# First-layer projections ahead of the global token, x loaded in halves, padding on VectorE, and a router product of weights, in a four-part transformer kernel

## The reference

```
x = x + attention0(layernorm(x))   # 16 heads of 64, windows of 128, plus one "global" part
x = x + memory(layernorm(x))       # router: top 8 of 512 stored values, scaled by a gate
x = x + attention1(layernorm(x))   # 16 heads of 8, all 2048 keys, rotary
x = x + experts(layernorm(x))      # main network and 2 of 8 experts per 128 tokens
```

## Time and profile before

| | us |
|---|---|
| median of 3 runs (1297.92, 1299.36, 1327.26) | 1299.36 |
| the profiled execution's own time | 1297.83 |
| its span in the trace | 1296.0 |
| busy: PE | 1230.3 (95%) |
| busy: DVE | 970.3 (75%) |
| busy: ACT | 883.0 (68%) |
| busy: POOL | 190.0 (15%) |

### The profile page before, as it was taken

How to read it: one execution, slowest core, us unless ns; L and a number is a source line. 1 busy time by engine, 2 the same in 40 slices (tenths; PEclk the granted TensorE clock), 3 DMA queues, 4 the chain that set the end, 5 groups by cost and what they waited for, 6 DMA issues and landing times. The chain is left out here.

```text
span 1296.0 us, 26594 instructions
## 1 busy us (share of the span) xinstructions
PE 1230.3 (95%) x10182; PEld 668.4 (52%) x10182; DVE 970.3 (75%) x1664; ACT 883.0 (68%) x2406; POOL 190.0 (15%) x369
## 2 busy tenths in 40 slices
PE   4999999999988878899999999999999999998999
PEld 3677777777874644333333333333333333334677
DVE  4566566666666878899999999999999999935300
ACT  1566666666657520388888888888888888885442
POOL 3233333333336040000000000010000000000100
PEclk8999999999998995699999999999999999999999
DMA  3200000000000031001110001100011000000100
GB/s 80 74 10 2 9 10 10 7 4 4 2 2 1 1 122 57 22 19 51 38 37 25 25 29 39 38 29 23 28 37 38 28 24 28 21 6 1 37 17 17
DMA packets 23051, 34.03 MB, mean 26 GB/s; under 512 B 6381, under 2 KB 16397, under 8 KB 20686
## 3 DMA queue, kind: packets, MB, share of 16 engines
q1 hardware_dynamic: 22926, 32.35, 7.5%
HBM read 24.86 MB, written 5.24 MB: 23 GB/s over the span
## 5 line engine op out<-in xcount | busy, mean ns | idle before, releaser
L1220 DVE TENSOR_REDUCE rowmax<-psum 128x1 f32<-128x1024 f32 x512 | 618.3, 1224 | 32.3 <-PE psum L1083 24.8
L1325 ACT ACTIVATE pb<-psum 128x512 f32<-128x512 f32 x1024 | 556.0, 595 | 82.6 <-PE psum L1125 61.7
L1083 PE MATMUL psum<-kf,qf 64*128 64x512 f32 x1024 | 389.7, 463 | 8.2 <-DVE rowmax L1220 6.5
L1125 PE MATMUL psum<-qf,kf 64*128 64x512 f32 x1024 | 377.1, 448 | 3.7 <-issue 2.6
L1110 PE MATMUL psum<-pb,vx 128*32 128x256 f32 x4096 | 327.9, 392 | 3.6 <-issue 3.6
L1125 PEld LDWEIGHTS psum<-qf,kf 64*128 64x128 f32 x1024 | 153.4, 186 | 212.6 <-ACT pb L1325 191.6
L1110 PEld LDWEIGHTS psum<-pb,vx 128*32 128x32 f32 x4096 | 81.4, 108 | 189.5 <-ACT pb L1325 94.8
L1083 PEld LDWEIGHTS psum<-kf,qf 64*128 64x128 f32 x1024 | 159.1, 193 | 31.1 <-DVE rowmax L1220 25.0
L532 ACT ACTIVATE pr<-psum,nmax 128x128 f32<-128x128 f32 x256 | 93.9, 367 | 114.1 <-DVE nmax L475 114.0
L570 POOL TENSOR_TENSOR pr<-pr,rtotal 128x256 f32<-128x256 f32 (+1 forms) x256 | 110.7, 454 | 238.5 <-DVE rtotal L483 238.5
L474 DVE TENSOR_REDUCE nmax<-psum 128x2 f32<-128x256 f32 x128 | 53.7, 420 | 65.1 <-PE psum L343 65.1
(11 more groups left out here) (216 smaller groups left out, 1374.6 us busy)
## 6 DMA issues: line engine op xcount, KB each, us to landing
qf<-q_parts SPq DMA_DIRECT2D x62, 128.0 KB
kf<-k_parts SPq DMA_DIRECT2D x62, 128.0 KB
k_parts<-parts SPq DMA_DIRECT2D x4, 512.0 KB, 3.5
q_parts<-parts SPq DMA_DIRECT2D x4, 512.0 KB, 4.1
cos<-cos_table SPq DMA_DIRECT2D x1, 1024.0 KB
sin<-sin_table SPq DMA_DIRECT2D x1, 1024.0 KB
sumsT<-acc SPq DMA_DIRECT2D x60, 16.0 KB
attT<-acc SPq DMA_DIRECT2D x60, 16.0 KB
```

What stands on the lines that cost most here:

```text
L1083: mm = nc.tensor.matmul(m.psum[:, M_B + (u % 2) * 2 + n % 2, :], qf[ROWS, b, t * P:(t + 1) * P], kf[ROWS, b, c * BANK:(c + 1) * BANK], sta ...
L1125: nc.tensor.matmul(m.psum[:, bank, :], kf[SCORES, b, t * P:(t + 1) * P], qf[SCORES, b, c * BANK:(c + 1) * BANK], start=True, stop=True).th ...
L1220: nc.vector.tensor_reduce(rowmax[:, g % 2, u // 2, u % 2:u % 2 + 1], m.psum[:, M_B + (u % 2) * 2:M_B + (u % 2) * 2 + 2, :].rearrange("p b ...
L1325: nc.scalar.activation(pb[:, s % 3, c, :], m.psum[:, bank_of[(s, c)], :], ACT.Exp, scale=SCALE).then_inc(exp_ready, 1)
```

## The change

Setup: x comes in two DMAs of 8 tiles, each with its own semaphore, and the first three weight tiles of pair 0 are loaded there; SP waits for none of them in this block. DVE waits for a half of x when it makes its statistics, SP for the small loads in ln0. DVE clears the padding of vz, gv and pr in the setup block; POOL gets one more memset (uw2_cols). Layer 0: q, k and v of bank 0 are projected before the second score matmul, q, k and v of bank 1 before the global projection; DVE's part moves accordingly. Memory block: TensorE turns q_proj once and multiplies it by the router weights, so that rq comes from xnT in one product per bank; the gate's hidden layer goes into four row groups of one bank, so that one Gelu takes it all and 4 products take the place of 16; rk comes first, and the scores wait for the part of rq that they read; DVE's bn_aggr and ACT's logarithm move behind rq and behind the first two score copies.

```diff
@@ ln_block
+            if first:
+                sp.wait_ge(m.small_loaded, 16 * 4)
...
             def stats(half):
+                if first:
+                    dve.wait_ge(m.x_loaded[half], 16)
@@ setup_block
-            sp.dma_start(m.x[:, :].rearrange("p (t d) -> p t d", d=D),
-                         a["L0_attn_x"][0].rearrange("(t p) d -> p t d", p=P)).then_inc(loaded, 16)
...
-            sp.wait_ge(loaded, 5 * 16)
+            for half in range(2):
+                own = slice(half * NT // 2, (half + 1) * NT // 2)
+                sp.dma_start(m.x[:, :].rearrange("p (t d) -> p t d", d=D)[:, own, :],
+                             a["L0_attn_x"][0].rearrange("(t p) d -> p t d", p=P)[:, own, :]).then_inc(m.x_loaded[half], 16)
...
+            for i, w in enumerate((a["L0_attn_wq"], a["L0_attn_wk"], a["L0_attn_wv"])):
+                sp.dma_start(m.w_cur[:, 0, i, :], w[:, 0:P]).then_inc(m.w_even_loaded, 16)
+
+        @block.vector
+        def _(dve):
+            for j in range(2):
+                nc.vector.memset(m.vz[:, :, j, :, (1 - j) * HD0:(2 - j) * HD0], 0.0)
+            nc.vector.memset(m.gv[:, :, :], 0.0)
+            nc.vector.memset(m.pr[:, :, 2 * WL:3 * P], 0.0)
...
+            nc.gpsimd.memset(m.uw2_cols[:, :], 0.0).then_inc(zeroed, 1)
@@ attn0_block, sync
-            for b in range(2):
-                load_w(b, b)
-                load_wo(b, b)
+            load_wo(0, 0)
+            load_w(1, 1)
+            load_wo(1, 1)
@@ attn0_block, tensor
-            pe.wait_ge(score_gelu, 1)
-            pe.wait_ge(ws2_spread, 1)
-            nc.tensor.matmul(m.psum[:, Y_B, 0:1], ws2r[:, :], gate_h[:, :], start=True, stop=True).then_inc(score_ready, 1)
-            pe.wait_ge(gtok_ready, 1)
...
             pe.wait_ge(w_loaded[0], 48)
-            project_globals(0)
             for c in range(NC):
-                if c == 0:
-                    pe.wait_ge(g_saved, 1)
-                else:
+                if c >= 1:
                     pe.wait_ge(q_saved, c)
                 project(0, c, "q", J_B)
...
                 project(0, c, "v", O_B)
+                if c == 0:
+                    pe.wait_ge(score_gelu, 1)
+                    pe.wait_ge(ws2_spread, 1)
+                    nc.tensor.matmul(m.psum[:, SCORE_B, 0:1], ws2r[:, :], gate_h[:, :], start=True, stop=True).then_inc(score_ready, 1)
+                if c == 1:
+                    pe.wait_ge(gtok_ready, 1)
+                    project_globals(0, T_B)
@@ attn0_block, vector
-            dve.wait_ge(zeroed, 1)
-            save_globals(0, 0)
             for c in range(NC):
                 save_keys(0, 0, c, Y_B)
                 save_values(0, 0, c, O_B)
+                if c == 0:
+                    choose_token()
+                if c == 1:
+                    save_globals(0, 0, T_B)
@@ attn0_block, gpsimd
-            nc.gpsimd.memset(gv[:, :, :], 0.0).then_inc(zeroed, 1)
-            for j in range(2):
-                other = slice((1 - j) * HD0, (2 - j) * HD0)
-                nc.gpsimd.memset(vz[:, :, j, :, other], 0.0).then_inc(zeroed, 1)
-            nc.gpsimd.memset(pr[:, :, 2 * WL:TW], 0.0).then_inc(zeroed, 1)
-            pool.wait_ge(zeroed, 4)
@@ memory_block, tensor
+            nc.tensor.transpose(m.psum[:, 5, 0:P], m.qpT[:, :], m.ident[:, :]).then_inc(product_ready, 1)
             for c in range(NC):
-                nc.tensor.matmul(m.psum[:, c, :], m.qpT[:, :], m.xnT[:, c * BANK:(c + 1) * BANK],
-                                 start=True, stop=True).then_inc(qy_ready, 1)
+                mm = nc.tensor.matmul(m.psum[c * UH:(c + 1) * UH, 4, :], m.uw1T[:, :], m.xnT[:, c * BANK:(c + 1) * BANK],
+                                      start=True, stop=True)
+            mm.then_inc(h1_ready, 1)
+            pe.wait_ge(product_saved, 1)
+            nc.tensor.matmul(m.psum[:, 6, 0:RD], qp[:, :], m.rwT[:, :], start=True, stop=True).then_inc(product_ready, 1)
+            nc.tensor.matmul(m.psum[0:RD, 7, :], m.rwT[:, :], m.akT[:, :], start=True, stop=True).then_inc(rq_ready, 1)
+            pe.wait_ge(product_saved, 2)
             for c in range(NC):
...
-                nc.tensor.matmul(m.psum[0:RD, c, :], m.rwT[:, :], qyT[:, c * BANK:(c + 1) * BANK],
+                nc.tensor.matmul(m.psum[0:RD, c, :], routed[:, :], m.xnT[:, c * BANK:(c + 1) * BANK],
                                  start=True, stop=True).then_inc(rq_ready, 1)
...
-            pe.wait_ge(rq_saved, NC + 1)
...
+                if s < 2:
+                    pe.wait_ge(rq_saved, s + 2)
+                elif s == 2:
+                    pe.wait_ge(rq_saved, NC + 1)
@@ memory_block, scalar
+            act.wait_ge(product_ready, 1)
+            nc.scalar.activation(qp[:, :], m.psum[:, 5, 0:P], ACT.Copy).then_inc(product_saved, 1)
+            act.wait_ge(product_ready, 2)
+            nc.scalar.activation(routed[:, :], m.psum[:, 6, 0:RD], ACT.Copy).then_inc(product_saved, 1)
+            act.wait_ge(h1_ready, 1)
+            nc.scalar.activation(h1T[:, :], m.psum[:, 4, :], ACT.Gelu, bias=m.ub1[:, 0:1]).then_inc(h1_saved, 1)
...
             save_scores(0)
             save_scores(1)
+            act.wait_ge(var_ready, NT)
+            nc.scalar.activation(logvar[:, :], mv[:, :, 1], ACT.Ln, bias=m.ones[:, 0:1], accum_out=logvar_sum[:, :])\
+                .then_inc(logvar_ready, 1)
@@ build
+        for c in range(NC):
+            rows = slice(c * UH, (c + 1) * UH)
+            loads += [(m.ub1[rows, :], column(a["L0_ffn_unc_b1"])), (m.uw2_cols[rows, c:c + 1], a["L0_ffn_unc_w2"])]
```

More of the change, by code:

```diff
@@ L49, with ln_block @@
     pass
-def ln_block(nc, m, tag, loads=()):
+def ln_block(nc, m, tag, first=False):
     with ExitStack() as ctx:
@@ L262, in attn0_block, with globals_in @@
         S_B, T_B, O_B, Y_B, J_B = 0, 4, 5, 6, 7
-        gk_ps = m.psum[:, J_B, 0:G0]
-        gv_ps = m.psum[0:2 * G0, J_B, P:2 * P]
+        HIDDEN_B, SCORE_B = 0, 1
+        def globals_in(bank):
+            return m.psum[:, bank, 0:G0], m.psum[0:2 * G0, bank, P:2 * P]
         def job(i, more):
@@ L300, in _, with project_globals @@
         def _(pe):
-            nc.tensor.matmul(m.psum[0:UH, J_B, 0:1], m.ws1[:, :], m.xnT[:, 0:1], start=True, stop=True).then_inc(score_hidden, 1)
-            pe.wait_ge(score_gelu, 1)
-            pe.wait_ge(ws2_spread, 1)
-            nc.tensor.matmul(m.psum[:, Y_B, 0:1], ws2r[:, :], gate_h[:, :], start=True, stop=True).then_inc(score_ready, 1)
-            pe.wait_ge(gtok_ready, 1)
-            def project_globals(b):
+            nc.tensor.matmul(m.psum[0:UH, HIDDEN_B, 0:1], m.ws1[:, :], m.xnT[:, 0:1], start=True, stop=True).then_inc(score_hidden, 1)
+            def project_globals(b, bank):
+                gk_ps, gv_ps = globals_in(bank)
                 nc.tensor.matmul(gk_ps, w_cur[:, b, 1, :], gtok[:, 0:G0], start=True, stop=True)
@@ L477, in step @@
                 if job(i, more) and job(i, more)[1:] == (0, "q"):
-                    save_globals(r, job(i, more)[0])
+                    save_globals(r, job(i, more)[0], J_B)
                 w = i - 1
@@ L514, in _ @@
             act.wait_ge(score_hidden, 1)
-            nc.scalar.activation(gate_h[:, :], m.psum[0:UH, J_B, 0:1], ACT.Gelu, bias=m.bs1[:, 0:1]).then_inc(score_gelu, 1)
+            nc.scalar.activation(gate_h[:, :], m.psum[0:UH, HIDDEN_B, 0:1], ACT.Gelu, bias=m.bs1[:, 0:1]).then_inc(score_gelu, 1)
             def save_queries(r, q, c):
@@ L646, in _ @@
                 if s == 1:
-                    for t in range(NT):
-                        mm = nc.tensor.matmul(m.psum[:, 5, t:t + 1], h1T[:, t * P:(t + 1) * P], m.uw2T[:, :],
+                    pe.wait_ge(h1_saved, 1)
+                    for i in range(TPB):
+                        mm = nc.tensor.matmul(m.psum[:, 5, i * NC:(i + 1) * NC], h1T[:, i * P:(i + 1) * P], m.uw2_cols[:, :],
                                               start=True, stop=True)
@@ L1593, in build @@
         m.wo_last = sb("wo_last", [P, D + 1])
+        m.uw2_cols = sb("uw2_cols", [P, NC])
         m.xnT_sum = sb("xnT_sum", [P, NC])
         m.psum = ctx.enter_context(nc.psum_tensor("psum", [P, 8, BANK], F32))
-        setup_block(nc, m, a)
-        ln_block(nc, m, "ln0")
+        m.x_loaded = [ctx.enter_context(nc.semaphore(f"x_half{i}_loaded")) for i in range(2)]
+        m.small_loaded = ctx.enter_context(nc.semaphore("small_loaded"))
+        m.w_even_loaded = ctx.enter_context(nc.semaphore("w_even_loaded"))
         def row(ap):
@@ L1634, in build, with lb @@
             loads.append((m.wo_last[c * VCOLS + HD1:c * VCOLS + 2 * HD1, 0:D], a["L1_attn_Wo"][(H1 - 1) * HD1:H1 * HD1, :]))
-        attn0_block(nc, m, a, loads)
+        with ExitStack() as layer:
+            def lb(name, shape, dt=F32):
+                return layer.enter_context(nc.sbuf_tensor(name, shape, dt))
+            m.w_cur, m.vz, m.gv, m.pr = lb("w_cur", [P, 2, 3, P]), lb("vz", [P, 2, 2, NT, P]), lb("gv", [P, 2, P]), lb("pr", [P, 4, 3 * P])
```

(3 more changed lines are left out.)

94 lines of the change are left out of this document (35 added, 59 removed).

## The result

The changed kernel takes 1285.05 us (median of 4 runs, 1284.34 to 1288.57) against 1300.99 for the kernel before on the same chip (4 runs); the ratio is 0.9897, 95% interval [0.9878, 0.9915]. By 2% the two kernels are the same, by the interval the changed one is about 1% faster. 1288 was forecast, 1282.5 to 1293.

What follows compares the result with a forecast made beforehand. Short serial chains at the starts of three stages, not PE's 95% share, were taken as the bound. 1.2 + 8.8 + 0.3 = 10.3 us off 1297.83 gave 1287.5; the typical run 0.5 above, 1288, range 1282.5 to 1293.

Steps and rivals of the forecast that it cites:

- Start: Setup block: without SP's wait for landings, DVE begins at about 7.3 instead of 8.45 us, a gain of 1.2 us.
- the list of SP's issues: Setup: SP's issuing ends last, 5.19 us plus half of x and three w at about 0.5 each, 7.2 us.
- the meeting: End of the setup block, where engines meet before the next block; costed at about 0.25 us.
- The padding: Setup: DVE's memsets, unheld by POOL, end between 5.0 and 7.0 us, 5.5 taken, and cost nothing.
- (b): Setup: POOL's setup holds DVE's padding, start -3.7 to -0.5 instead of +1.2, so 1290 to 1293; chance 0.13.
- Attention 0: First matmul to first step: the new list sums to 11.7 us against 20.49, a gain of 8.8 us.
- The covers: Attention 0: TensorE's 2.64 us of bank 1 covers DVE's token choice; without that cover it would cost 1.6 us.
- (c): Attention 0: the projections run at 1.2 GHz, the gain there falls to 1.6 us, 1295; chance 0.05.
- Router: Memory block: scores 3.5 us earlier, but POOL holds the gate; gain 0.3 us, between -1.0 and +4.2.
- (a): Router's gate: POOL doesn't hold L727, the router keeps its 3.5 us and perhaps 0.7, 1284; chance 0.17.
- the hidden layer costed as L623's 3.67: Router, TensorE's list before the scores: the hidden layer has as many columns as L623, so 3.67 us.
- (d): Router's loop stays at the low clock, 2.0 us more per tile, 1316 over all 14 tiles; chance 0.03.

Runs made afterwards that it cites:

- e1: The changed kernel with POOL's clearing of qf and kf put behind DVE's gate arithmetic; 1278.85 us, ratio to before 0.9847.
- e8: The changed kernel with the two held gate operations written as SCALAR_TENSOR_TENSOR with a second SBUF operand, POOL's order left alone; 1280.83 us, ratio to before 0.9865.
- e12: e9 with the third block's row loads issued some 10 us later, behind the loads for the scores; 1288.27 us, ratio to before 0.9928.
- e5: The kernel before with the padding cleared by DVE in the setup block and nothing else; 1297.73 us, ratio 0.9987.
- e2: The kernel before with POOL's clearing of qf and kf begun only when the gate arithmetic is done; 1299.85 us, ratio 1.0016.
- e3: The kernel before with the new memory block and its loads alone; 1290.02 us, ratio 0.9946.
- e9: The changed kernel with 29 more matrix multiplications in TensorE's program, before its wait for the log variance; 1290.88 us, ratio to before 0.9938.
- e11: The kernel before with the tiles and loads of the new memory block, TensorE's program untouched; 1301.29 us, ratio 1.0016.
- e6: The changed kernel with the padding back on POOL at the start of attention 0; 1282.68 us, ratio to before 0.9878.
- e10: The kernel before with 32 FP32 products more in TensorE's program, in its own memory block; 1307.37 us, ratio 1.0064.
- e7: The changed kernel with x in one load, still without SP's wait; 1285.27 us, ratio to before 0.9904.

## Why the prediction was right, and where not

*Start.* Sized at 1.2, measured 2.06. The step that failed is the list of SP's issues, 7.2 us: the three w cost 0.48 each, as sized, but the extra half of x added 0.17 and not 0.5 (1.08 against 0.91), and the issue of ws1 took 1.26 where the list kept its 2.03. SP ended at 5.95, and POOL's end at 5.99 became the bound, at the 2.0 that the prediction named for this case; in e1, e8 and e12 SP's end, at 6.05 to 6.12, was the later one. The prediction's own terms, 7.2 + 0.25 for the meeting, give 7.45 and a gain of 1.0, not 1.2.

*The padding.* DVE's memsets were to end between 5.0 and 7.0 us, with 5.5 taken. They ended at 5.69 without being held, so rival (b) falls.

*Attention 0.* Sized at 8.8, measured 8.51. The list was 11.7 and became 11.98, because three of the banks took 2.71 to 2.72 and the first 2.80, not 2.64. The covers held: nothing in TensorE waited for the token. The clock was at its upper level, so (c) falls. By e5 the padding carries about 2.3 of it, and the order with the earlier weights the rest.

*Router.* Sized at 0.3, measured 0.5, by the mechanism forecast: both gate operations held by POOL, the second until kf is cleared. e1, e2 and e8 show it, and (a) falls. But the first exp was due 402.7 - 386.51 = 16.2 us after the block's start and came after 13.2. The step that failed is the hidden layer costed as L623's 3.67: its four products fill four groups of 32 partitions of one bank and took 1.07 together. So the gate met POOL 3 us sooner, at the start of qf and not at its end, and paid 3.63 instead of 0.6; as kf ends the hold either way, the sum stayed. What the prediction put at 0.6 of 3.5 saved was 0.5 of 6.5. That is in part luck: in e3 DVE came 0.3 us earlier against POOL's list, caught the gap between POOL's memsets, and the block took 60.6 us, 3.5 less than before. (d) falls as well: the last 14 exps run from 401.5 to 434.0, 2.50 us apart, though the loop was entered after a standstill.

*What was missing.* Of the 13.4 us, 2.2 have no term in the sum. 4.4 us came in the loop of attention 1, through the number of TensorE's instructions ahead of it, as e9 to e11 show; 2.6 were lost between the layer norm and the first exp there (87.4 to 90.0 us over the kernels, with either memory block), which stays open. The stretch behind the last exp gave the other 0.4. The step that failed here is costing unchanged code at nothing: its 2.2 outweigh the 0.9 by which the start was undersized. That 4.4 and 2.6 cancelled down to 2.2 is luck, and the range had room for it.

## What to carry to other kernels

A TENSOR_SCALAR of 16 columns on DVE paid for the whole of a 3.5 us memset on POOL here: when a chain is moved forward, look at what the other engine does at its new time, and order the long memset behind it or write the operation in a form that isn't held. Read a change stage by stage, because totals mixed a loss of 1.2 with a stroke of luck of 2.8 (e6) and a loss of 13 with a gain of 4 (e10). In a loop like this one, whose turn of 768 instructions takes three program packets, code far ahead of it can make it slower or faster: here by 4.4 us in 16 turns.

## What was not expected of the hardware

- Four FP32 products of 512 columns, written to four groups of 32 partitions of one bank, took 1.07 us against 3.62 in the kernel before one after the other: 3.4 times as fast.
- POOL leaves 0.06 us between two memsets. A DVE operation that had waited 0.3 us went through in it in e3 and e6 (0.33 us in all); one that came 0.02 to 0.03 us before it missed it in the changed kernel, e7, e9 and e12 (3.62 to 3.63 us).
- DVE's two memsets of 2048 columns are listed with 1.76 us each but start 2.14 apart, in every kernel that has them.
- Gaps of TensorE of up to 1.24 us stand in 33 of the 49 heads whose program packet comes 1.0 to 2.8 us behind the turned maxima, and in none of the 161 where it comes 3.3 us behind or more (the 0.24 at the end of every head left aside).
